# Attention over picked rows in the second layer: scores in four row tiles of TensorE, scaling on GpSimd, another order of turning and projecting

## The chip, the cores and the metric

One core of a Trainium2 chip runs the whole program. The metric is the device time of one execution in microseconds; where a median is given, it is over several executions of the same kernel. The engines are TensorE (PE, with its weight loads as PEld), VectorE (DVE), ScalarE (ACT), GpSimd (POOL) and the queue of SyncE (SP), which issues most DMA transfers.

## The reference

Two samples of 128 rows with 512 columns pass through two layers of a perceiver: cross-attention, attention, feed-forward, and the same again. Six stages follow one another. The change touches one, the cross-attention of the second layer, which picks one context row for each row of x and then attends over the picked rows:

```python
def _L1_xattn_ref(q, kv, Wq, Wkv, Wc):        # q: 2 x 128 x 512, kv: 2 x 2048 x 512, 16 heads of 32
    qp = jnp.einsum('bld,ed->ble', q, Wq)
    scores = jnp.einsum('bld,bmd->blm', qp, kv)
    idx = jnp.argmax(scores, axis=-1)
    mem = jnp.take_along_axis(kv, idx[..., None], axis=1)      # the picked rows
    mkv = jnp.einsum('bld,ed->ble', mem, Wkv)                  # one key and one value of 32, shared by the heads
    mk, mv = jnp.split(mkv, 2, axis=-1)
    qh = qp.reshape(b, l, h, dh).transpose(0, 2, 1, 3)
    logits = jnp.einsum('bhld,bmd->bhlm', qh, mk) * scale
    attn = jax.nn.softmax(logits, axis=-1)
    out = jnp.einsum('bhlm,bmd->bhld', attn, mv)
    return jnp.einsum('bld,ed->ble', out.transpose(0, 2, 1, 3).reshape(b, l, d), Wc)

x = x + _L1_xattn_ref(_layernorm(x, axis=-1), ctx_1024, L1_xattn_Wq, L1_xattn_Wkv, L1_xattn_Wc)
```

## The kernel before, in words

Each engine has its own program, written out by hand in the order in which it runs; semaphores join them. No planner moves anything, so the order of calls in `cross1_pe`, `cross1_act`, `cross1_dve` and in the GpSimd and SyncE blocks is the order on the chip. Everything in this stage runs in float32; such a matmul leaves two records in the trace, a transposing one leaves one.

The stage works on two samples, b = 0 and 1. For each it does the following.

1. The scores over 2048 context rows go to four PSUM banks, DVE finds the largest (`pick_dve`), and GpSimd fetches the picked rows with an indirect DMA (L2692).
2. TensorE turns them (`turn_mem`, L2035), `copy_mem` (L2141, on ACT) brings them to SBUF, and `project_mem` makes the key (L2041) and the value (L2045). The key weights stand four times side by side, so that the key appears in each of the four groups of 32 partitions.
3. `spread_mk` (DVE, L2214) multiplies the key with a mask, so that `mkz` holds four blocks, each with the key in one group of 32 partitions and zeros in the others. With it `logits` (L2053) makes the scores of four heads in one matmul of 128 partitions by 512 columns, one bank for each group of four heads (heads 4j to 4j+3 in bank j), and signals after each bank.
4. For each bank j, DVE takes the maxima (`largest_la`, L2220 and L2221), ACT the exponentials with their sums (`exp_la`, L2151), DVE the reciprocals (L2226) and the scaling (L2227), both in `scale_la`. TensorE turns the scaled weights (`turn_la`, L2059), a copy brings them back (`copy_laT`: DVE L2231 for sample 0, ACT L2168 for sample 1), and `mix_mem` (L2065) multiplies with the value.
5. `out_x1` (L2069) multiplies with the output weights, which lie in the ring block `BLK_X1 + 1`, and DVE adds the result to x (L2267, L2271).

`keep_clock` (L275) are matmuls without use, put where TensorE would wait. The ring has four blocks of 1 MB, which SP refills from `stream` through `dma_block` (L222) once `blk_used` says that the one before is spent. The context comes back to SBUF through eight transfers that GpSimd issues (L2689). Behind this stage comes `linear_pe` (L2305), and then the feed-forward with its large matmuls (L2470, L2487, L2488).

Of the kernel before, what the change touches and what calls it, by code (L numbers as in the profile page):

```python
# [16 lines left out]
P = 128  # L17
B = 2
D = 512
C = D // P  # L20
# [6 lines left out]
DK = D // H  # L27
# [6 lines left out]
RING = 4  # L34
# [81 lines left out]
def build(nc, x, ctxT, ctx_rows, wq, wk, wv, wo, stream, small, cols, rows, consts, out):  # L116
# [6 lines left out]
    with ExitStack() as ctx:  # L123
# [43 lines left out]
        def view(at, *shape, one_pass=False):  # L167
            n = int(np.prod(shape))
            assert at + n <= ARENA, (at, shape)
            if one_pass:  # L170
                assert at // ARENA_R == (at + n - 1) // ARENA_R, (at, shape)
                v = arena_r[at // ARENA_R][:, at % ARENA_R:at % ARENA_R + n]
            else:
                v = arena[:, at:at + n]
            if len(shape) == 1:
                return v
            letters = "abcd"[:len(shape)]
            return v.rearrange(f"p ({' '.join(letters)}) -> p {' '.join(letters)}",
                               **dict(zip(letters[:-1], shape[:-1])))
# [1774 lines left out]
        mkz = view(19456, B, 4, P)  # L1954
# [30 lines left out]
        mkz_ready = sem("mkz_ready")  # L1985
        mv_ready = sem("mv_ready")
# [13 lines left out]
        X1_BANK = (5, 6)  # L2000
        CTX_SPLITS = ctx_count(B - 1, KB - 1, 0)
        LA_SCALE = float(1.0 / np.sqrt(DK).astype(np.float32))

        def cross1_pe(pe):
# [44 lines left out]
            def logits(b):  # L2049
                pe.wait_ge(mkz_ready, b + 1)  # L2050
                pe.wait_ge(mv_ready, b + 1)
                for j in range(C):
                    nc.tensor.matmul(psum[:, PICK_BANK[b] + j, :], qpT[:, j, b * P:(b + 1) * P], mkz[:, b, :, :],  # L2053
                                     start=True, stop=True).then_inc(la_filled, 1)
# [30 lines left out]
            turn_mem(1)  # L2085
            project_mem(1)
            logits(1)
            for j in range(C):
                turn_la(0, j)
            for j in range(C):  # L2090
                last = mix_mem(0, j, psum[:, PICK_BANK[0], j * P:(j + 1) * P])
            last.then_inc(x1o_filled, 1)
            need(pe, BLK_X1 + 1)
# [17 lines left out]
        def cross1_act(act):  # L2111
# [30 lines left out]

            def copy_mv(b):
                act.wait_ge(mkv_filled, 2 * b + 2)
                nc.scalar.copy(mvt[:, b, :], psum[:, MV_BANK[b], 0:DK]).then_inc(mv_ready, 1)
# [8 lines left out]

            copy_mem(0)
            copy_mv(0)
            exp_la(0, 0)
            exp_la(0, 1)
            copy_mem(1)
            exp_la(0, 2)  # L2160
# [19 lines left out]
            copy_x1o(C - 1)  # L2180

        def cross1_dve(dve):
# [29 lines left out]
            def spread_mk(b):  # L2212
                dve.wait_ge(mkv_filled, 2 * b + 1)
                nc.vector.tensor_tensor(mkz[:, b, :, :], per_row(psum[:, MK_BANK[b], 0:P], 4),  # L2214
                                        per_elem(K_("headmask", 0, 4), P), ALU.mult).then_inc(mkz_ready, 1)

            def largest_la(b, j):
                dve.wait_ge(la_filled, C * b + j + 1)
                heads = slice(4 * j, 4 * j + 4)
                link(dve, nc.vector.reduce_max(lm[:, b, heads], bank4(PICK_BANK[b] + j), AX.X))  # L2220
                nc.vector.tensor_scalar(nlm[:, b, heads], lm[:, b, heads], -LA_SCALE, None, ALU.mult).then_inc(lm_ready, 1)  # L2221

            def scale_la(b, j):
                dve.wait_ge(la_exp, C * b + j + 1)
                heads = slice(4 * j, 4 * j + 4)
                link(dve, nc.vector.reciprocal(ls[:, b, heads], ls[:, b, heads]))  # L2226
                nc.vector.tensor_tensor(la[:, b, heads, :], la[:, b, heads, :], per_elem(ls[:, b, heads], P), ALU.mult).then_inc(la_ready, 1)  # L2227
# [19 lines left out]
            spread_mk(0)  # L2247
            for j in range(C):
                largest_la(0, j)
            scale_la(0, 0)  # L2250
            spread_mk(1)
            scale_la(0, 1)
            largest_la(1, 0)
            largest_la(1, 1)
            scale_la(0, 2)
            largest_la(1, 2)
            largest_la(1, 3)
            scale_la(0, 3)
            for j in range(C):
                copy_laT(0, j)  # L2260
            scale_la(1, 0)
            dve.wait_ge(x1o_filled, 1)
            nc.vector.tensor_copy(x1oT[:, :, 0:P], bank4(PICK_BANK[0])).then_inc(x1o_ready, 1)
            for j in range(1, C):
                scale_la(1, j)
# [322 lines left out]
        def _(sp):  # L2588
# [74 lines left out]
            with sp.Fori(0, E) as e:  # L2663
                for q, (u, i) in enumerate(MOE_ORDER):
                    dma_block(sp, ds(e * NEXP + (BLK_MOE + 3 * u + i), 1), BLK_MOE + q, used=e * NEXP + (BLK_MOE + q - RING + 1))
            turns = (NBLK - BLK_X1) // RING
            with sp.Fori(0, turns) as i:
                for s in range(RING):
                    dma_block(sp, ds(i * RING + (BLK_X1 + s), 1), BLK_X1 + s, used=i * RING + (BLK_X1 + s - RING + 1))
# [8 lines left out]
        def _(gp):  # L2678
# [11 lines left out]
            for b in range(B):  # L2690
                gp.wait_ge(picked, b + 1)
                gp.indirect_dma_start(out=mem[:, b, :], out_offset=None, in_=ctx_rows,  # L2692
                                      in_offset=bass.IndirectOffsetOnAxis(ap=pick[b][:, :], axis=0)).then_inc(mem_arrived[b], 16)
# [102 lines left out]
```

## Time and profile before

| | us |
|---|---|
| median of three runs | 1342.53 |
| the three runs | 1336.44, 1345.71, 1342.53 |
| profiled execution, device time | 1338.34 |
| profiled execution, span of the trace | 1336.6 |
| PE busy in the span | 1301.4 |
| DVE busy | 916.7 |
| ACT busy | 718.3 |
| GpSimd busy | 28.6 |

The span is that of the trace, the device time also holds what lies around it. Busy times come from single records; the end of a matmul in them is modelled. The changed code works between about 1012 us and 1046 us of the span.

### The profile page before, as it was taken

The numbers are of one execution on the slowest core, as the hardware profiler recorded it, in microseconds if no ns is written. First come the engines' busy times: TensorE is split into PE (matmuls) and PEld (weight loads), VectorE is DVE, ScalarE is ACT, GpSimd is POOL, SyncE is SP. The second block draws the span as 40 slices with busy tenths as digits, with TensorE's granted clock in tenths as the row PEclk, the third lists the DMA queues.
The fourth block names the chain that finished last, engine by engine and source line by source line (L and its number), as shares of the span: only waits on it lengthen the run. The fifth ranks groups of instructions, "written<-read, shape, count | busy, mean of one in ns | idle before, by whom it ended". The sixth has DMA issues, their size and how long they took to land.

```text
span 1336.6 us, 23941 instructions
## 1 busy us (share of the span) xinstructions
PE 1301.4 (97%) x9964; PEld 1104.9 (83%) x9964; DVE 916.7 (69%) x1199; ACT 718.3 (54%) x888; POOL 28.6 (2%) x24
## 2 busy tenths in 40 slices
PE   9999999999999999998999999999988999999998
PEld 8899998989999997776677888888765789888887
DVE  4566566776565665675688989989868577555554
ACT  5544444554444443482377777777654445666552
POOL 0000000000000000002000000000011010000000
PEclk9999999999999999997899999999989999999999
DMA  8101010321010011201069999999970145455552
GB/s 298 37 23 45 23 37 21 107 75 37 21 37 26 23 64 64 95 34 66 33 225 343 349 361 350 344 351 349 364 269 16 64 158 187 174 190 191 189 191 90
DMA packets 50367, 197.72 MB, mean 148 GB/s; under 512 B 12128, under 2 KB 20576, under 8 KB 30560
## 3 DMA queue, kind: packets, MB, share of 16 engines
q1 hardware_dynamic: 47936, 187.41, 39.0%
q0 software_dynamic: 2336, 8.91, 1.8%
q8 instruction: 75, 1.23, 0.4%
q14 instruction: 20, 0.16, 0.0%
HBM read 195.78 MB, written 0.52 MB: 147 GB/s over the span
## 4 chain that ended last, share of the span: by engine, by line
PE 88%; DVE 6%; ACT 2%; DMA 2%; issue 2%; SPq 0%; POOL 0%; ACTq 0%; DVEq 0%
PE psum L465 13%; PE psum L435 13%; PE psum L2487 9%; PE psum L1683 8%; PE psum L492 5%; PE psum L2488 4%; PE psum L1706 4%; PE psum L517 4%; PE psum L1686 4%; PE psum L2470 3%; PE psum L1053 2%; PE psum L1709 2%; PE psum L2496 2%; PE psum L476 1%; PE psum L1720 1%
## 5 line engine op out<-in xcount | busy, mean ns | idle before, releaser
L1752 DVE TENSOR_TENSOR arena_r<-ring,arena_r 128x2048 fp32r<-128x2048 f32 x96 | 219.7, 2290 | 29.5 <-ACT arena_r L1746 29.2
L465 PE MATMUL psum<-ring_r,arena_r 128*128 128x256 f32 x1536 | 198.1, 287 | 0.6 <-DVE ring_r L300 0.6
L1746 ACT CAST arena_r<-ring 128x2048 fp32r<-128x2048 f32 x96 | 183.4, 1914 | 14.4 <-PE psum L1686 11.1
L465 PEld LDWEIGHTS psum<-ring_r,arena_r 128*128 128x128 f32 x1536 | 188.6, 191 | 1.3 <-DVE ring_r L300 1.0
L435 PE MATMUL psum<-arena_r 128*128 128x512 f32 x768 | 184.0, 394 | 0.8 <-ACT arena_r L809 0.4
L2487 PE MATMUL psum<-arena_r 128*128 128x512 f32 x512 | 177.7, 393 | 1.1 <-DVE arena_r L2562 1.1
L435 PEld LDWEIGHTS psum<-arena_r 128*128 128x128 f32 x768 | 141.5, 188 | 33.3 <-issue 1.6
L2488 PE MATMUL psum<-arena_r 128*128 128x256 f32 x512 | 142.6, 279 | 0.0
L2441 DVE TENSOR_TENSOR arena_r<-ring,arena_r 128x2048 fp32r<-128x2048 f32 x43 | 98.6, 2293 | 62.1 <-ACT arena_r L2436 62.1
L1683 PE MATMUL psum<-arena_r 128*128 128x512 f32 x512 | 129.5, 395 | 1.3 <-issue 1.3
L2487 PEld LDWEIGHTS psum<-arena_r 128*128 128x128 f32 x512 | 95.9, 187 | 22.9 <-DVE arena_r L2562 1.3
L1683 PEld LDWEIGHTS psum<-arena_r 128*128 128x128 f32 x512 | 94.2, 188 | 20.4 <-issue 1.7
L795 ACT COPY arena<-psum 128x1024 f32<-128x1024 f32 x64 | 61.7, 1016 | 89.6 <-PE psum L492 89.6
L300 DVE TENSOR_TENSOR arena_r<-arena,arena_r 128x2048 fp32r<-128x2048 f32 (+4 forms) x34 | 52.1, 1538 | 80.8 <-ACT arena_r L766 52.3
L2436 ACT CAST arena_r<-ring 128x2048 fp32r<-128x2048 f32 x44 | 84.0, 1910 | 30.0 <-PE psum L2470 19.7
L2488 PEld LDWEIGHTS psum<-arena_r 128*128 128x128 f32 x512 | 96.5, 188 | 0.0
L650 DVE TENSOR_TENSOR arena<-arena,psum 128x1024 f32<-128x1024 f32 x64 | 75.2, 1216 | 24.8 <-PE psum L506 24.8
L787 ACT COPY ring<-psum 128x512 f32<-128x512 f32 x64 | 37.2, 581 | 77.8 <-PE psum L465 77.8
L802 ACT ACTIVATE arena<-arena 128x1024 f32<-128x1024 f32 x64 | 66.3, 1058 | 21.0 <-DVE arena L650 19.7
L630 DVE TENSOR_TENSOR arena<-arena 128x512 f32<-128x512 f32 x124 | 69.3, 559 | 4.2
L1686 PE MATMUL psum<-arena_r 128*128 128x512 f32 x256 | 68.5, 390 | 0.0
L492 PEld LDWEIGHTS psum<-arena 64*128 64x128 f32 x1024 | 59.7, 188 | 9.9 <-issue 9.1
(345 smaller groups left out, 1902.7 us busy)
## 6 DMA issues: line engine op xcount, KB each, us to landing
ring<-in_stream SPq DMA_DIRECT2D x151, 1024.0 KB, 4.9
arena<-in_ctxT POOLq DMA_DIRECT2D x8, 1024.0 KB, 11.9
arena<-in_ctxT SPq DMA_DIRECT2D x7, 1024.0 KB, 8.1
arena<-in_wk SPq DMA_DIRECT2D x16, 256.0 KB, 3.2
wv_in<-in_wv SPq DMA_DIRECT2D x8, 512.0 KB, 3.6
arena<-in_wq SPq DMA_DIRECT2D x16, 256.0 KB, 2.7
arena<-in_wk SPq DMA_DIRECT2D x16, 128.0 KB, 3.2
arena<-in_wo SPq DMA_DIRECT2D x2, 1024.0 KB, 6.9
```

The source lines that it names most:

```text
L435: last = nc.tensor.matmul(bank, wk_sb[wp][:, c, w], cx[xp][kb][:, c, :], start=c == wp == xp == 0, stop=c == C - 1 and xp == 1)
L465: last = nc.tensor.matmul(bank[:, q * T:(q + 1) * T], cx[xp][kc // 4][:, c, kc % 4 * P:(kc % 4 + 1) * P], wv_sb[wp][:, c, :], start=c == w ...
L492: last = nc.tensor.matmul(psum[:, 2 * half + kc // 4, kc % 4 * P:kc % 4 * P + P], kT[j % 2][a:a + 64, k0:k0 + P], qT[a:a + 64, j % 2, half ...
L650: nc.vector.tensor_tensor(part, part, per_row(psum[:, SPREAD_BANK, 0:P], KC // 2), ALU.subtract).then_inc(shifted, 1)
L1683: nc.tensor.matmul(out, xg[xp][:, c, e, :], hi[:, c, :], start=c == xp == 0, stop=False)
L1686: last = nc.tensor.matmul(out, xg[0][:, c, e, :], lo[:, c, :], start=False, stop=c == C - 1)
L1746: nc.scalar.copy(mwhi[p % MB], ring[k % RING][:, :]).then_inc(moe_hi, 1)
L1752: nc.vector.tensor_tensor(mwlo[p % MB], ring[(BLK_MOE + p) % RING][:, :], mwhi[p % MB].bitcast(fp32), ALU.subtract).then_inc(moe_lo if p < ...
L2436: nc.scalar.copy(whi[j % 2], ring[k % RING][:, :]).then_inc(w_hi, 1)
L2441: nc.vector.tensor_tensor(wlo[j % 2], ring[(BLK_W12 + j) % RING][:, :], whi[j % 2].bitcast(fp32), ALU.subtract).then_inc(w_lo, 1)
L2487: nc.tensor.matmul(psum[:, 4 + s, :], w[0][:, c, :], src[:, :, c, :], start=c == 0, stop=False)
L2488: last = nc.tensor.matmul(psum[:, 4 + s, 0:T], w[1][:, c, :], src[:, 0, c, :], start=False, stop=c == FC - 1)
```

## The change

The mask is gone. `copy_mk` (ACT) copies the key from PSUM as it is (128 x 128), and `logits` makes 16 matmuls, each with 32 partitions of the query and of the key and 128 columns: row group j of the array writes to bank j, head group c to its column block. So bank j now holds the heads j, 4+j, 8+j and 12+j, and `la_filled` is raised once, after all 16. As the heads stand in another order, the rows of the output weights must too: SP loads block `BLK_X1 + 1` in four transfers of 32 partitions, each with runs of 512 numbers in place of 2048, and the first turn of its last loop is written out for that.

The scaling goes from DVE to GpSimd (`cross1_pool`), the reciprocals stay on DVE (`sums_la`). The copy of the second sample's picked rows goes from ACT to DVE. On TensorE `turn_la(0, 0)` comes ahead of `project_mem(1)` and `turn_la(0, 1)` ahead of `logits(1)`; the wait for the output weights moves ahead of `mix_mem` of sample 0.

```diff
             def logits(b):
-                pe.wait_ge(mkz_ready, b + 1)
-                pe.wait_ge(mv_ready, b + 1)
-                for j in range(C):
-                    nc.tensor.matmul(psum[:, PICK_BANK[b] + j, :], qpT[:, j, b * P:(b + 1) * P], mkz[:, b, :, :],
-                                     start=True, stop=True).then_inc(la_filled, 1)
+                pe.wait_ge(mkv_ready, 2 * b + 2)
+                for c in range(C):
+                    for j in range(4):
+                        r = tile_rows(j)
+                        last = nc.tensor.matmul(psum[:, PICK_BANK[b] + j, c * P:(c + 1) * P], qpT[r, c, b * P:(b + 1) * P], mk[r, b, :],
+                                                start=True, stop=True)
+                last.then_inc(la_filled, 1)
...
             logits(0)
             turn_mem(1)
+            turn_la(0, 0)
             project_mem(1)
+            turn_la(0, 1)
             logits(1)
-            for j in range(C):
+            for j in range(2, C):
                 turn_la(0, j)
+            need(pe, BLK_X1 + 1)
+            pe.wait_ge(wo_arrived, WO_PARTS * 16)
             for j in range(C):
                 last = mix_mem(0, j, psum[:, PICK_BANK[0], j * P:(j + 1) * P])
             last.then_inc(x1o_filled, 1)
-            need(pe, BLK_X1 + 1)
             turn_la(1, 0)
...
+            def copy_mk(b):
+                act.wait_ge(mkv_filled, 2 * b + 1)
+                nc.scalar.copy(mk[:, b, :], psum[:, MK_BANK[b], 0:P]).then_inc(mkv_ready, 1)
...
             copy_mem(0)
+            copy_mk(0)
             copy_mv(0)
-            exp_la(0, 0)
-            exp_la(0, 1)
-            copy_mem(1)
-            exp_la(0, 2)
+            for j in range(3):
+                exp_la(0, j)
+            copy_mk(1)
             copy_mv(1)
             exp_la(0, 3)
...
+        def cross1_pool(gp):
...
+            for b in range(B):
+                for j in range(C):
+                    heads = slice(4 * j, 4 * j + 4)
+                    gp.wait_ge(ls_ready, C * b + j + 1)
+                    nc.gpsimd.tensor_tensor(la[:, b, heads, :], la[:, b, heads, :], per_elem(ls[:, b, heads], P), ALU.mult).then_inc(la_ready, 1)
...
-            def scale_la(b, j):
+            def sums_la(b, j):
                 dve.wait_ge(la_exp, C * b + j + 1)
                 heads = slice(4 * j, 4 * j + 4)
-                link(dve, nc.vector.reciprocal(ls[:, b, heads], ls[:, b, heads]))
-                nc.vector.tensor_tensor(la[:, b, heads, :], la[:, b, heads, :], per_elem(ls[:, b, heads], P), ALU.mult).then_inc(la_ready, 1)
+                nc.vector.reciprocal(ls[:, b, heads], ls[:, b, heads]).then_inc(ls_ready, 1)
...
+            dma_block(sp, BLK_X1, BLK_X1, used=BLK_X1 - RING + 1)
+            sp.wait_ge(blk_used, BLK_X1 - RING + 2)
+            for i in range(4):
+                part = stream[BLK_X1 + 1].rearrange("(j d) (c n) -> d j c n", d=DK, c=C)[:, :, i, :]
+                sp.dma_start(block(BLK_X1 + 1)[tile_rows(i), :, :], part).then_inc(wo_arrived if i else blk_arrived[(BLK_X1 + 1) % RING], 16)
+            for k in range(BLK_X1 + 2, BLK_X1 + RING):
+                dma_block(sp, k, k, used=k - RING + 1)
             turns = (NBLK - BLK_X1) // RING
-            with sp.Fori(0, turns) as i:
+            with sp.Fori(1, turns) as i:
```

On TensorE, from the end of the picking to the mixing of sample 0, there stood before (L2035 turns picked rows, L2041 and L2045 project, L2053 makes scores, L2059 turns weights, L2065 mixes):

```order
L2053 MATMUL psum<-arena 128x512 x4
L2035 MATMUL psum<-cst,arena 128x128 x4
L2041 MATMUL psum<-arena,sml 128x128 x4
L2045 MATMUL psum<-sml,arena 128x32 x4
L2053 MATMUL psum<-arena 128x512 x4
L2059 MATMUL psum<-cst,arena 128x128 x16
```

and now stands, with L2055 for the scores, L2036 and L2062 for the turning, L2042 and L2046 for the projecting:

```order
L2055 MATMUL psum<-arena 128x128 x16
L2036 MATMUL psum<-cst,arena 128x128 x4
L2062 MATMUL psum<-cst,arena 128x128 x4
L2042 MATMUL psum<-arena,sml 128x128 x4
L2046 MATMUL psum<-sml,arena 128x32 x4
L2062 MATMUL psum<-cst,arena 128x128 x4
L2055 MATMUL psum<-arena 128x128 x16
L2062 MATMUL psum<-cst,arena 128x128 x8
```

Two of the four groups of turned weights of sample 0 moved up, one ahead of the projecting of sample 1 and one ahead of its scores.

On DVE, from the last maxima of sample 0 on, the rows before were these (L2214 spreads the key, L2226 and L2227 scale, L2231 copies turned weights, L2263 copies the mixed values of sample 0):

```order
L2226 RECIPROCAL ls<-ls 128x4
L2227 TENSOR_TENSOR arena<-arena,ls 128x512
L2214 TENSOR_TENSOR arena<-psum,col 128x512
L2226 RECIPROCAL ls<-ls 128x4
L2227 TENSOR_TENSOR arena<-arena,ls 128x512
L2220 TENSOR_REDUCE lm<-psum 128x4
L2221 TENSOR_SCALAR nlm<-lm 128x4
L2220 TENSOR_REDUCE lm<-psum 128x4
L2221 TENSOR_SCALAR nlm<-lm 128x4
L2226 RECIPROCAL ls<-ls 128x4
L2227 TENSOR_TENSOR arena<-arena,ls 128x512
```

and now they are these (L2246 takes the reciprocals, L2235 copies the picked rows of sample 1, L2250 copies turned weights, L2240 and L2241 take the maxima):

```order
L2246 RECIPROCAL ls<-ls 128x4
L2235 COPY arena<-psum 128x4x128
L2246 RECIPROCAL ls<-ls 128x4 x2
L2250 COPY arena<-psum 128x512 x2
L2246 RECIPROCAL ls<-ls 128x4
L2240 TENSOR_REDUCE lm<-psum 128x4
L2241 TENSOR_SCALAR nlm<-lm 128x4
L2240 TENSOR_REDUCE lm<-psum 128x4
```

The scalings left this engine, and the maxima of sample 1 now stand behind the reciprocals of the last bank of sample 0 and behind two copies.

## Rows read from the trace of the kernel before

**Rows 1.** The page: busy time by engine, then the engines' shares of the chain.

```profile
PE 1301.4 (97%) x9964; PEld 1104.9 (83%) x9964; DVE 916.7 (69%) x1199; ACT 718.3 (54%) x888; POOL 28.6 (2%) x24
PE 88%; DVE 6%; ACT 2%; DMA 2%; issue 2%; SPq 0%; POOL 0%; ACTq 0%; DVEq 0%
```

**Rows 2.** Chain that ended last, 1017 to 1046: start, length, work.

```profile
1017.42 0.70 DVE lm L2220
...
1018.36 2.90 ACT arena L2151 x16
1021.25 0.48 ACT arena L2141
...
1021.78 1.16 PE psum L2041 x8
1022.94 0.83 PE psum L2045 x8
...
1023.79 0.19 ACT mvt L2145
...
1024.12 1.11 PE psum L2053 x2
...
1025.25 0.70 DVE lm L2220
...
1030.22 2.40 DVE arena L2231 x4
...
1032.73 0.70 DVE arena L2227
...
1033.57 1.09 PE psum L2059 x4
1034.66 1.71 PE psum L2069 x2
...
1036.83 0.86 PE psum L2069 x2
...
1038.63 0.86 PE psum L2069 x2
...
1043.06 2.79 PE psum L2069 x6
```

**Rows 3.** Timeline, 1015 to 1021: start, length, engine, line, work.

```profile
1015.38 0.98 POOL L2692 DMA_INDIRECT arena<-in_ctx_rows,pick  x1 [5.43 <-DVE pick L2210]
...
1016.29 3.67 PE L2053 MATMUL psum<-arena 128*128 128x512 f32 x8
...
1018.28 0.69 DVE L2220 TENSOR_REDUCE lm<-psum 128x4 f32<-128x512 f32 x1
...
1019.80 0.60 PE L2035 MATMUL psum<-cst,arena 128*128 128x128 f32 x4
```

**Rows 4.** Timeline of the mixer stage: 16 matmuls of 32 partitions, four row groups.

```profile
614.96 1.17 PE L1083 MATMUL psum<-arena 32*128 32x128 f32 x32
...
622.80 1.70 PE L1083 MATMUL psum<-arena 32*128 32x128 f32 x32 [2.73 <-DVE arena L1373]
```

**Rows 5.** Groups on GpSimd, by form: busy time, mean ns of one.

```profile
L1379 POOL TENSOR_TENSOR arena<-arena 128x1024 f32<-128x1024 f32 x4 | 9.3, 2346 | 67.5 <-ACT arena L1334 67.5
...
L2695 POOL TENSOR_TENSOR arena_r<-ring,arena_r 128x2048 fp32r<-128x2048 f32 x1 | 4.5, 4547 | 55.1 <-ACT arena_r L2436 55.1
```

**Rows 6.** Windows: length, busy PE, PEld, DVE, ACT, POOL; then PEclk, DMA share, GB/s.

```profile
973.00:974.00 1.00, 0.00 (x0) 0.00 (x0) 0.93 (x4) 0.50 (x3) 1.00 (x2) 1.00 0.11 33
...
975.00:976.00 1.00, 0.36 (x1) 0.36 (x2) 0.28 (x1) 1.00 (x2) 1.00 (x3) 0.50 0.97 279
...
980.00:981.00 1.00, 1.00 (x4) 0.82 (x3) 0.81 (x1) 0.00 (x0) 0.00 (x0) 0.50 1.02 381
...
1028.00:1032.00 4.00, 2.56 (x31) 1.60 (x28) 3.90 (x10) 3.87 (x23) 0.00 (x0) 1.00 0.00 0
1032.00:1036.00 4.00, 3.37 (x22) 1.79 (x23) 3.86 (x11) 0.58 (x1) 0.00 (x0) 0.61 0.00 0
```

More of the change, by code:

```diff
@@ L1953, in build @@
         memT = view(18432, C, T)
-        mkz = view(19456, B, 4, P)
+        mk = view(19456, B, P)
         la = view(20480, B, H, P)
@@ L1984, in build @@
         mkv_filled = sem("mkv_filled")
-        mkz_ready = sem("mkz_ready")
-        mv_ready = sem("mv_ready")
+        mkv_ready = sem("mkv_ready")
+        ls_ready = sem("ls_ready")
         la_filled = sem("la_filled")
@@ L2000, in build @@
         X1_BANK = (5, 6)
+        WO_PARTS = 2 + 3
         CTX_SPLITS = ctx_count(B - 1, KB - 1, 0)
@@ L2141, in copy_mem @@
                 nc.scalar.copy(memT[:, :, b * P:(b + 1) * P], bank4(MEM_BANK[b])).then_inc(memT_ready, 1)
+            def copy_mk(b):
+                act.wait_ge(mkv_filled, 2 * b + 1)
+                nc.scalar.copy(mk[:, b, :], psum[:, MK_BANK[b], 0:P]).then_inc(mkv_ready, 1)
             def copy_mv(b):
                 act.wait_ge(mkv_filled, 2 * b + 2)
-                nc.scalar.copy(mvt[:, b, :], psum[:, MV_BANK[b], 0:DK]).then_inc(mv_ready, 1)
+                nc.scalar.copy(mvt[:, b, :], psum[:, MV_BANK[b], 0:DK]).then_inc(mkv_ready, 1)
             def exp_la(b, j):
@@ L2180, in cross1_act @@
             copy_x1o(C - 1)
+        def cross1_pool(gp):
+            for b in range(B):
+                gp.wait_ge(picked, b + 1)
+                gp.indirect_dma_start(out=mem[:, b, :], out_offset=None, in_=ctx_rows,
+                                      in_offset=bass.IndirectOffsetOnAxis(ap=pick[b][:, :], axis=0)).then_inc(mem_arrived[b], 16)
+            for b in range(B):
+                for j in range(C):
+                    heads = slice(4 * j, 4 * j + 4)
+                    gp.wait_ge(ls_ready, C * b + j + 1)
+                    nc.gpsimd.tensor_tensor(la[:, b, heads, :], la[:, b, heads, :], per_elem(ls[:, b, heads], P), ALU.mult).then_inc(la_ready, 1)
         def cross1_dve(dve):
@@ L2210, in pick_dve, with copy_mem @@
                 nc.vector.tensor_scalar(pick[b][:, :], at8[b][:, 0:1], b * CTX, None, ALU.add).then_inc(picked, 1)
[L2212 to L2215, printed above, removed]
+            def copy_mem(b):
+                dve.wait_ge(memT_filled, b + 1)
+                nc.vector.tensor_copy(memT[:, :, b * P:(b + 1) * P], bank4(MEM_BANK[b])).then_inc(memT_ready, 1)
             def largest_la(b, j):
-                dve.wait_ge(la_filled, C * b + j + 1)
+                dve.wait_ge(la_filled, b + 1)
                 heads = slice(4 * j, 4 * j + 4)
@@ L2246, in cross1_dve @@
             pick_dve(1)
-            spread_mk(0)
             for j in range(C):
                 largest_la(0, j)
[L2250 to L2258, printed above, removed]
+            sums_la(0, 0)
+            copy_mem(1)
+            sums_la(0, 1)
+            sums_la(0, 2)
+            copy_laT(0, 0)
+            copy_laT(0, 1)
+            sums_la(0, 3)
             for j in range(C):
-                copy_laT(0, j)
-            scale_la(1, 0)
+                largest_la(1, j)
+            copy_laT(0, 2)
+            copy_laT(0, 3)
+            sums_la(1, 0)
             dve.wait_ge(x1o_filled, 1)
@@ L2264, in cross1_dve @@
             for j in range(1, C):
-                scale_la(1, j)
+                sums_la(1, j)
             dve.wait_ge(x1_proj, 2)
@@ L2689, in _ @@
                     gp.dma_start(ctxT_sb[b][kb], ctxT[b][:, :, kb * 512:(kb + 1) * 512]).then_inc(ctx_back[(b * KB + kb) // 2], 16)
[L2690 to L2693, printed above, removed]
+            cross1_pool(gp)
             gp.wait_ge(w_hi, 1)
```

## The prediction

> **What bounds the kernel now.** The page says first where a gain could lie at all: PE is busy in 97% of the span and holds 88% of the chain that ended last [rows 1]. The changed stage is some 34 us of 1336.6, from 1012 to 1046, so nothing in it can move the total by more than a small part. Then I read the chain through this stage [rows 2]. It changes hands at each step: maxima on DVE, exponentials on ACT (two banks in 2.90 us), the copy of sample 1's picked rows (1021.25), projecting (1021.78, 1022.94), the value's copy (1023.79), scores of sample 1 (1024.12), maxima (1025.25), then DVE without a break until the scaling at 1032.73. From 1033.57 to 1045.85 (1043.06 + 2.79) TensorE runs alone, turning and multiplying for sample 1. So two thirds of the stage is latency, one third PE's own work. Last I read the clock by windows [rows 6]: full in 1028 to 1032, 0.61 in 1032 to 1036.
>
> **The change part by part.** I follow sample 0 and then sample 1 through the new order, with the durations of the old trace.
>
> *Scores.* The old four matmuls took 3.67 us, and DVE began on the first bank 1.13 us after their start (1016.29 to 1017.42) [rows 2, 3]. The new form, 16 matmuls of 32 partitions into four banks, stands in the mixer: 1.17 us for the 16 (32 records) [rows 4]. With about 0.07 us to the next engine all four banks are there after 1.24 us. PE gets 2.5 us back per sample, but DVE takes a bank each 0.86 us (1017.42 to 1018.28) [rows 2, 3], as fast as PE made them before. Sample 0's maxima start at 1017.53 and end at 1020.97: no gain, 0.1 us lost.
>
> *The mask.* `spread_mk` was one DVE pass over a bank, about 0.7 us by the others of that size [rows 2], made while PE was still making the value and ACT copying it, so it lay beside other work; `copy_mk` takes its place there. Worth nothing for the chain.
>
> *Picked rows of sample 1.* PE turned them at 1019.80 [rows 3], behind the scores. The issue of the gather ends at 1016.36 (1015.38 + 0.98) [rows 3], and the rows had landed when PE came for them, so the landing lies between; I take 1018.9. The exact time is of no weight, since DVE, which copies now, is in the maxima until 1020.97; it then takes a reciprocal (0.2) and copies a bank (0.7): 1021.87. Before, ACT's copy let PE go at 1021.78. Nothing gained.
>
> *Turning ahead of projecting.* PE now waits at `turn_la(0, 0)` with `project_mem(1)` queued behind it, and behind that ACT's `copy_mv(1)` and with it `exp_la(0, 3)`. It waits for GpSimd's first scaling. GpSimd's two-input operation takes 2346 ns at 1024 columns and 4547 at 2048 [rows 5], that is 2.15 ns a column and 0.15 us fixed: 1.25 us at 512. From the reciprocal at 1021.15: done at 1022.45, turned by 1022.95. So projecting starts at 1022.95 in place of 1021.78: 1.2 us late. From its start to that of the scores it took 2.34 us (1021.78 to 1024.12) [rows 2]: scores at 1025.3.
>
> *Maxima of sample 1.* They need the banks (1026.5) and stand behind `sums_la(0, 3)`, whose exponentials start after `copy_mv(1)` at 1025.15 and take 1.5: 1026.9, where it was 1025.25. Then DVE has four maxima (3.44), two copies of turned weights (1.2, half of the four in 2.40 [rows 2]) and a reciprocal (0.2): 4.9 us, to 1031.8. Before, the same point was reached 7.4 us after 1025.25, at 1032.6, since three scalings and four copies lay between. This is the gain: 2.5 us less on DVE, of which 1.65 is spent on the late start. GpSimd scales in 1.25, and `turn_la(1, 0)` starts at 1033.2 where it was 1033.57 [rows 2]: 0.4 us early.
>
> *Tail.* Turning, multiplying and mixing for one group take PE 1.80 us at full clock (1036.83 to 1038.63 [rows 2]); GpSimd delivers each 1.25 us, so PE stays the bound and the tail keeps its length. At full clock throughout it would be shorter: `out_x1` took 1.71 at first and 0.86 later, the first turning 1.09 in place of about 0.6 [rows 2], so 1.2 us are the low clock's [rows 6].
>
> *Output weights in four transfers.* They go out where the DMA engines have a share of only 0.11 soon after (973 to 974) [rows 6], before the last six context transfers, and are needed at 1031. Cover: some 50 us. If it were gone, some of the block's 1 MB at 0.38 MB/us (380 GB/s) [rows 6] would stand on the path, up to 2.6 us.
>
> *The clock.* This is what the latency sum leaves out. PE's work in the middle shrinks by 5 us. From 1017.5 to 1022.5 it has only the 0.6 us of turning left [rows 3]. Two stretches show what follows. PE idle at 973 to 974 had the clock at 0.50 by 975, and still there at 980 with PE fully busy [rows 6]. And 1028 to 1032, with PE busy 2.56 of 4 us, was followed by 0.61. So I expect the clock to fall near 1021, ahead of `project_mem(1)`. At half, projecting (1.16 + 0.83) takes 2.0 more, the scores 1.70 in place of 1.17 [rows 4]: `turn_la(1, 0)` moves from 1033.2 to about 1035.3, or 1.7 later than before. Against that, a clock that has come back by the tail saves up to 1.2 there.
>
> The Trainium skill, "TensorE: Matmul & The Clock Gate", Part 4, says that a transpose does not count as PE being busy in the way a matmul does. By that rule the turning in the gap does not hold the clock and the fall is surer; if turning counted in full, nothing above would change but the chance.
>
> **The sum.** With the clock as before: -0.4 us. With a fall in the gap: +1.7, less 0 to 1.2 in the tail, so +0.5 to +1.7, and up to +2.9 if the low clock also reaches 1.2 us deeper into the tail than it did. I take the second case at +1.0: profiled execution 1338.34 + 1.0 = 1339.3. The three timed runs lie 9 us apart; their middle is 1342.53, the mean of all four executions is 1340.8. From the latter I forecast 1342, no change that can be measured (about 1% or 13 us is what a measurement tells from none).
>
> **The rivals.**
>
> *The clock holds.* Then -0.4, or -1.6 if it holds in the tail too: 1340. For it: in 1028 to 1032 PE was idle for 1.44 of 4 us and the clock stayed full throughout [rows 6]. Against: the new gap is three times that.
>
> *GpSimd becomes the bound, ending slower.* The scaling reads its second operand spread over 128 columns, a form that is not in the trace. If it took the 2.35 us of a 1024-column one, the first turning and with it projecting would come 1.1 late, `turn_la(1, 0)` 1.1 more, and the tail would be paced by GpSimd: three times 2.35 - 1.80, 1.6 us. Together +3.8 on the sum: 1345. It decides from 1.80 us for one scaling. The linear price of 1.25 [rows 5] speaks against.
>
> The Trainium skill, "GPSIMD Engine Reference", Engine selection, says to keep elementwise work of two inputs on VectorE, since GpSimd is about twice slower. By that factor DVE's 0.69 would become an estimate of 1.4 us, 0.15 above mine, still under 1.80; the rule's warning holds for each operation but not for this place, where DVE is the fuller engine.
>
> *The row groups don't run side by side.* Then 16 matmuls take the old 3.7 us and the one signal comes at their end: maxima of sample 0 start 2.5 late, everything on behind it, and the same for sample 1. +4 to +5: 1346. The mixer's 1.17 us [rows 4] speaks against; it is the same shape and bank pattern.
>
> *More is gained than the chain shows.* PE's 5 us of freed work could count only if PE were what the middle waits for, and it is not. The most that the stage could give back is the 2.5 us of DVE and the 1.2 of the clock: 1338.
>
> **How the numbers follow.** Chances: fall of the clock in the gap, +0.5 to +2.9, 0.55; clock holds, 0.27; GpSimd paces, 0.08; row groups serial, 0.03; more gained, 0.07. All of them lie within 6 us of 1341, well inside 1%, so "same" gets 0.95; the rest, 0.03 faster and 0.02 slower, is for something outside this stage that no row shows. The range takes the lowest run (1336.4) less 1.6 and the highest (1345.7) plus 2.9: 1335 to 1349; three runs' spread makes nearly all of it.
>
> **What would show it.** Right: the new scores at about 1.2 us with four row groups overlapping; GpSimd's scaling at 1.2 to 1.4 us; `project_mem(1)` waiting for the turning behind GpSimd, starting some 10.4 us after `turn_mem(0)`; a granted clock under 1 between the scores of sample 0 and those of sample 1; the stage (from `turn_mem(0)` to the last addition) within 3 us of its 33.3. Wrong: a stage more than 3 us shorter, which would mean that DVE's order costs less than I sum; scaling above 1.8 us; or a difference outside 1012 to 1046, above all in the context transfers before 983, which the four new transfers could delay.

## The result, and the profile after

The changed kernel is slower by a third of a per cent: 1347.28 us median of 15 runs (1344.61 to 1350.16) against 1342.53 us of 15 runs of the kernel before (1336.44 to 1349.17), ratio 1.0032 with a 95% interval of 1.0019 to 1.0044. That is inside the range that was given, but the interval leaves out "no change", and no move was forecast.

The two profiled executions lie 10.2 us apart (spans 1336.6 and 1346.8), twice the difference of the medians. So the first step was to cut both spans at landmarks and to see which pieces belong to the change.

| piece (us) | before | after | difference |
|---|---|---|---|
| start to the first matmul of the experts (L1612) | 668.5 | 669.8 | 1.3 |
| from there to the first turning of picked rows | 344.1 | 346.7 | 2.6 |
| the stage, from that turning to the last addition to x | 33.3 | 36.2 | 2.9 |
| middle of the feed-forward (L2487, L2505 to the last product) | 177.6 | 181.0 | 3.4 |

A second trace of the kernel before (n1, below) has 180.9 us for the last row with the same code, and 666.6 for the first. The first and the last row are therefore differences between executions, and 5.5 us are left for the change, close to the 4.75 us of the medians. The trace of before is the odd one: over all 14 traces the last row is 181.0 in twelve (180.97 to 180.99), 179.2 in e7 and 177.6 in this one alone.

The stage first. The chain that ended last in the changed kernel answers to [rows 2] (start, length, work):

```profile
1021.50 0.70 DVE lm L2240
...
1024.95 1.04 POOL arena L2201
...
1026.04 1.11 PE psum L2062 x4
1027.16 1.71 PE psum L2042 x8
1028.86 1.55 PE psum L2046 x8
1030.41 0.91 PE psum L2062 x4
1031.32 2.06 PE psum L2055 x32
...
1033.40 0.70 DVE lm L2240
...
1036.69 1.19 DVE arena L2250 x2
...
1038.04 1.05 POOL arena L2201
...
1039.13 1.12 PE psum L2062 x4
1040.25 1.71 PE psum L2072 x2
...
1042.81 1.71 PE psum L2072 x2
...
1049.89 2.79 PE psum L2072 x6
```

The reader is to see two things. GpSimd's scaling (L2201) stands on the chain twice, at 1.04 us each. And every TensorE step of the chain between 1026 and 1043 is stretched: the key takes 1.71 us where it took 1.16, the value 1.55 for 0.83, turning 1.1, the scores of sample 1 2.06, and two `out_x1` (L2072) take 1.71 where only one did.

The windows say why (columns as in [rows 6]; the seventh number after the length is the granted clock as a share):

```profile
1020.00:1024.00 4.00, 1.44 (x34) 0.98 (x32) 2.39 (x7) 2.89 (x11) 0.45 (x1) 1.00 0.25 70
1024.00:1028.00 4.00, 3.07 (x13) 2.68 (x14) 2.48 (x7) 2.73 (x16) 2.70 (x3) 0.50 0.00 0
1028.00:1032.00 4.00, 4.00 (x29) 3.67 (x31) 0.65 (x1) 1.82 (x10) 0.37 (x1) 0.50 0.00 0
1032.00:1036.00 4.00, 3.38 (x52) 2.71 (x44) 2.71 (x9) 1.70 (x11) 1.04 (x1) 0.72 0.00 0
1036.00:1040.00 4.00, 1.95 (x20) 1.23 (x21) 2.77 (x8) 4.00 (x24) 1.53 (x2) 0.70 0.00 0
1040.00:1044.00 4.00, 4.00 (x10) 1.80 (x8) 0.18 (x1) 1.19 (x3) 2.54 (x3) 0.50 0.02 4
```

After 1020 to 1024, where PE is busy for 1.44 of 4 us, the clock is at half (1.2 in place of 2.4 GHz) for ten microseconds; it comes back, PE idles again around 1036, and it halves a second time, into the tail. Before, there was one such stretch [rows 6].

The timeline of the changed kernel shows the new scores and the gap behind them (start, length, engine, line; idle time before and its end in brackets):

```profile
978.47 1.22 PE L275 MATMUL psum<-cst 128*128 128x256 f32 x2 [4.65 <-issue]
...
1020.26 1.17 PE L2055 MATMUL psum<-arena 32*128 32x128 f32 x32
...
1024.33 1.11 PE L2036 MATMUL psum<-cst,arena 128*128 128x128 f32 x4 [2.89 <-DMA arena<-in_ctx_rows,pick]
```

The scores take 1.17 us, to the digit what the mixer's took [rows 4]; then TensorE has nothing for 2.89 us. The first line is the other piece: TensorE stands still for 4.65 us near 975, 3.17 in the trace before, ahead of an instruction that waits for no semaphore. "Issue" means that the profile names no releaser.

### The profile page after: what moved, and what is told of

Its sections match the earlier page's. It is cut to its first block, busy times and chain, and to the rows that moved or that the text cites. A ratio compares the mean times of both kernels' runs of the same rounds, so it can differ in the third digit from the quotient of the medians.

```text
span 1346.8 us, 24025 instructions
## 1 busy us (share of the span) xinstructions
PE 1307.5 (97%) x10012; PEld 1111.6 (83%) x10012; DVE 910.9 (68%) x1190; ACT 718.4 (53%) x889; POOL 36.7 (3%) x32
## 4 chain that ended last, share of the span: by engine, by line
PE 88%; DVE 6%; ACT 2%; DMA 2%; issue 2%; POOL 0%; SPq 0%; ACTq 0%; DVEq 0%
PE psum L465 13%; PE psum L435 13%; PE psum L2505 9%; PE psum L1683 8%; PE psum L492 5%; PE psum L2506 4%; PE psum L1706 4%; PE psum L517 4%; PE psum L1686 4%; PE psum L2488 3%; PE psum L1053 2%; PE psum L1709 2%; PE psum L2514 2%; PE psum L476 1%; PE psum L1720 1%
## 5 line engine op out<-in xcount | busy, mean ns | idle before, releaser
L2505 PE MATMUL psum<-arena_r 128*128 128x512 f32 x512 | 181.0, 399 | 1.1 <-DVE arena_r L2580 1.1
L2505 PEld LDWEIGHTS psum<-arena_r 128*128 128x128 f32 x512 | 96.2, 188 | 25.3 <-DVE arena_r L2580 1.2
## 6 DMA issues: line engine op xcount, KB each, us to landing
arena<-in_ctxT POOLq DMA_DIRECT2D x8, 1024.0 KB, 13.1
```

Source lines behind the costliest of these rows:

```text
L2505: nc.tensor.matmul(psum[:, 4 + s, :], w[0][:, c, :], src[:, :, c, :], start=c == 0, stop=False)
```

## The experiments

All traces, cut in the same way (us, to within 0.1; the stage ends where the last addition starts). "Wait" is that idle time near 975; "rows" the time from L1612 to the first turning of picked rows; "value" and "maxima" when the last matmul of sample 1's value and its last maximum start, from the stage's start; "tail" from the first `out_x1` to the last addition.

| trace | load in | wait | rows | stage | value | maxima | tail |
|---|---|---|---|---|---|---|---|
| before | one | 3.17 | 344.1 | 33.3 | 10.9 | 15.9 | 11.4 |
| n1, before again | one | 3.05 | 345.3 | 32.1 | 10.9 | 16.0 | 10.6 |
| after | four narrow | 4.65 | 346.7 | 36.2 | 13.5 | 19.3 | 12.7 |
| e1 | one | 3.20 | 343.9 | 36.0 | 13.5 | 19.3 | 12.4 |
| e2 | four narrow | 4.38 | 347.9 | 32.1 | 10.9 | 16.0 | 10.6 |
| e3 | one | 3.06 | 345.1 | 31.1 | 11.9 | 16.7 | 10.5 |
| e4 | one | 3.62 | 345.1 | 35.1 | 12.8 | 18.9 | 10.6 |
| e5 | one | 3.57 | 345.4 | 33.3 | 12.5 | 17.8 | 10.5 |
| e6 | one | 2.81 | 345.2 | 33.9 | 13.1 | 18.9 | 11.2 |
| e7 | one | 3.12 | 347.1 | 31.8 | 11.6 | 16.4 | 11.2 |
| e8 | one | 3.07 | 345.1 | 30.1 | 10.9 | 15.7 | 10.5 |
| e9 | one | 3.59 | 345.2 | 31.0 | 11.5 | 16.6 | 10.5 |
| e10 | four of all partitions | 3.26 | 344.1 | 32.1 | 10.9 | 15.9 | 10.6 |
| e11 | four narrow, long runs | 4.93 | 349.1 | 32.0 | 10.8 | 15.9 | 10.6 |

### e1: the changed kernel with one transfer

The rows of the output weights are put in the new order when the arrays are laid out, and SP's loop is the old one.

```diff
-    mats += [a["L1_xattn_Wq"].T, a["L1_xattn_Wc"].T]
+    wc = a["L1_xattn_Wc"].T
+    mats += [a["L1_xattn_Wq"].T, wc.reshape(C, 4, DK, D).transpose(1, 0, 2, 3).reshape(D, D)]
...
-            pe.wait_ge(wo_arrived, WO_PARTS * 16)
...
-            for i in range(4):
-                part = stream[BLK_X1 + 1].rearrange("(j d) (c n) -> d j c n", d=DK, c=C)[:, :, i, :]
-                sp.dma_start(block(BLK_X1 + 1)[tile_rows(i), :, :], part)...
...
-            with sp.Fori(1, turns) as i:
+            with sp.Fori(0, turns) as i:
```

> The changed kernel, with the output weights' rows put in the new order when the arrays are laid out, so that one transfer of 1 MB loads the block and the loop of the queue is the old one. Load theory: of the loss of 4.7 us the four transfers hold some 2.5 (the wait of TensorE before its turning at about 975 us goes from 4.65 back to 3.2, and the context arrives 1 us sooner), so 1344.5 to 1345.5. Clock theory alone: the loss stays, 1347, and the stage from turning the picked rows to the last addition stays at 36.2 us. Drift theory (the rest lies in the feed-forward, in code that did not change): 1347 with a feed-forward middle near 181 us again.

Measured: 1346.79 us median, ratio to the kernel before 1.0009 (0.9992 to 1.0026). The interval takes in no change, and the 12 runs are scattered (1337.22 to 1348.64). The ratio has come down from 1.0032, but its interval overlaps that of the changed kernel, and the median lies only 0.5 us under 1347.28, where the load theory had some 2.5. So the times do not settle it. The trace is plainer: the wait is 3.20, the rows piece 343.9, and the stage is 36.0, as in the changed kernel.

### e2: the kernel before with four transfers

```diff
+            pe.wait_ge(wo_arrived, WO_PARTS * 16)
...
+            dma_block(sp, BLK_X1, BLK_X1, used=BLK_X1 - RING + 1)
+            sp.wait_ge(blk_used, BLK_X1 - RING + 2)
+            for i in range(4):
+                part = stream[BLK_X1 + 1].rearrange("(j d) (c n) -> d j c n", d=DK, c=C)[:, :, i, :]
+                sp.dma_start(block(BLK_X1 + 1)[tile_rows(i), :, :], part)...
...
```

The arrays are laid out so that the same block results.

> The kernel before, with the block of output weights loaded by four transfers of 32 partitions and the array laid out so that the block is the same. Load theory: slower than before by 1.5 to 3 us (1344 to 1345.5), rate of the DMA engines near 230 GB/s for several us before 972, the stage itself unchanged at 33.2. Clock theory alone: as before, 1342.5.

Measured: 1346.01 us, ratio 1.0014 (0.9997 to 1.0031). Wait 4.38, rows piece 347.9, stage 32.1. The interval just takes in no change. In the trace the transfers bring the wait with them into the old kernel, and leave the stage alone.

### n1: the kernel before once more

No edit.

> The kernel before, once more, for its trace. If the middle of the feed-forward (177.6 us before, 181.0 in the changed kernel, same code) differs from run to run by a few us, the drift theory holds and those 3.4 us are not of the change; if it is 177.6 again, they are.

Measured: 1339.88 us, middle of the feed-forward 180.9 us. The drift theory holds: those 3.4 us are not of the change. The trace also shows the old stage at 32.1 in place of 33.3, with the clock full throughout. e2, e10 and e11 have 32.0 to 32.1 too, so the low stretch on which [rows 6] rests was in one of five traces of the old stage.

### e10 and e11: which feature of the four transfers is slow

Both are the kernel before. e10 cuts the block by columns (all 128 partitions, runs of 2 KB), e11 by partitions (32 each, runs of 8 KB).

```diff
+                part = stream[BLK_X1 + 1][:, i * D:(i + 1) * D]                 # e10
+                dst = block(BLK_X1 + 1)[:, i, :]
...
+                part = stream[BLK_X1 + 1][tile_rows(i), :]                      # e11
+                dst = ring[(BLK_X1 + 1) % RING][tile_rows(i), :]
```

> The kernel before, with the block of output weights in four transfers of all 128 partitions and 512 numbers each: short runs of 2 KB, all partitions. If the short runs make the load slow, TensorE's wait near 975 us is 4.4 us as with the four transfers of 32 partitions, and the engines move under 300 GB/s for some us before; if not, 3.1 us and about 400 GB/s.

> The kernel before, with the block of output weights in four transfers of 32 partitions, each row whole: 8 KB runs. If writing to 32 partitions at a time makes the load slow, TensorE's wait near 975 us is 4.4 us and the rate is under 300 GB/s; if not, 3.1 us and about 400 GB/s.

Measured: wait 3.26 and 4.93, rows piece 344.1 and 349.1; one execution each, 1344.35 and 1349.42. The window 970 to 975, first of e10, with 388 GB/s at a DMA share of 1.00:

```profile
970.00:975.00 5.00, 4.59 (x20) 3.25 (x19) 1.44 (x2) 1.97 (x2) 0.00 (x0) 1.00 1.00 388
```

and of e11, with the engines as busy and 225 GB/s:

```profile
970.00:975.00 5.00, 4.59 (x20) 3.24 (x19) 1.24 (x2) 1.97 (x2) 0.00 (x0) 1.00 1.04 225
```

The changed kernel has 229 in the same place, e1 422 (the windows of those two):

```profile
968.00:973.00 5.00, 4.59 (x19) 3.25 (x19) 1.82 (x3) 1.97 (x2) 0.00 (x0) 1.00 1.10 229
```

```profile
970.00:975.00 5.00, 4.59 (x20) 3.16 (x18) 2.40 (x4) 1.97 (x2) 0.00 (x0) 1.00 1.02 422
```

It is the 32 partitions, not the short runs. The Trainium skill, "SBUF — State Buffer", Door 1, says that DMA bandwidth depends on how many of the 16 ports a transfer's partitions reach, and that a group of 32 reaches eight of them. By that rule the rate should halve, and it nearly does, 388 to 225; the order in which four such transfers share the ports is not in the traces.

What TensorE waits for near 975 can be read from the `--dma` view, which counts packets by queue and has queues of the kind "instruction" (packets, MB, share of the engines' time). Seven microseconds around the wait, 970.7 to 977.7 in the kernel before and 972 to 979 in the changed one, give the same two lines:

```profile
q8 instruction: 1, 0.02, 1.0%
q14 instruction: 1, 0.01, 0.3%
```

The packet of queue 8 has 16 KB and takes 1.1 us. One falls into the wait in each of the 14 traces, and TensorE's next matmul starts 1.42 to 1.46 us after its end. What differs is when it starts: 0.3 to 1.1 us after TensorE stopped in the eleven traces with a wide load, 1.8 to 2.4 us in the three with a narrow one (in the changed kernel TensorE stopped at 973.82 and the packet started at 975.92; before, 972.47 and 973.13).

### e3: fillers in both gaps

e1 with matmuls without use where TensorE stood idle:

```diff
             logits(0)
+            pe.wait_ge(picked, 2)
+            keep_clock(pe, 3, 5)
             turn_mem(1)
+            keep_clock(pe, 3, 3)
             turn_la(0, 0)
...
             for j in range(C):
+                if j == 2:
+                    keep_clock(pe, 5, 4)
                 last = mix_mem(0, j, psum[:, PICK_BANK[0], j * P:(j + 1) * P])
             last.then_inc(x1o_filled, 1)
+            keep_clock(pe, 5, 2)
```

> As the kernel with one transfer, and matmuls without use in the gaps that the change opened on TensorE: 5 and 3 around the turning of the second sample's picked rows, 4 and 2 around the end of the mixing of sample 0. Clock theory: granted clock 1.0 through the stage, projecting of sample 1 back at 2.0 us in place of 3.3, the stage at 31.5 to 33 us in place of 36.2, total 3 to 4.5 us under the run with one transfer. Rival (the stage is held by GpSimd and the order, not by the clock): the stage within 1 us of 36.2. Rival (the fillers stand in the way themselves): longer than 36.2.

Measured: 1342.72 us, ratio to the kernel before 0.9993 (0.9980 to 1.0007), 4.1 us under e1's median in the same job (by the two ratios, 2.1); stage 31.1. The windows of e1, two of them with the clock at 0.50:

```profile
1019.00:1023.00 4.00, 1.44 (x34) 1.25 (x35) 2.77 (x7) 2.91 (x12) 0.12 (x1) 0.88 0.26 70
1023.00:1027.00 4.00, 3.07 (x15) 2.67 (x14) 2.10 (x7) 2.35 (x14) 3.09 (x3) 0.50 0.00 0
1027.00:1031.00 4.00, 4.00 (x35) 3.67 (x37) 0.87 (x2) 1.86 (x10) 0.05 (x1) 0.50 0.00 0
```

and of e3, whose stage begins at the same 1015.1:

```profile
1019.00:1023.00 4.00, 3.39 (x42) 2.66 (x42) 2.79 (x7) 2.91 (x12) 0.13 (x1) 1.00 0.26 70
1023.00:1027.00 4.00, 3.82 (x29) 3.62 (x30) 2.08 (x7) 2.59 (x15) 3.07 (x3) 1.00 0.00 0
1027.00:1031.00 4.00, 3.15 (x51) 2.46 (x54) 2.68 (x7) 2.30 (x14) 1.04 (x1) 1.00 0.00 0
```

The edit adds matmuls and one wait to TensorE and nothing else, and takes 4.9 us off the stage. This is the clearest of the runs: the low clock cost all that the stage lost and more. The clock is not a matter of the profiled execution alone: the granted clock over the whole program is 0.981 on average in the timed runs of the changed kernel and of e1, 0.986 in those of e3 and of the kernel before. The gain in time, 2.1 to 4.1 us, is less sharp than that of the stage.

### e7: fillers in the first gap alone

e3 without the second pair:

```diff
             for j in range(C):
-                if j == 2:
-                    keep_clock(pe, 5, 4)
                 last = mix_mem(0, j, psum[:, PICK_BANK[0], j * P:(j + 1) * P])
             last.then_inc(x1o_filled, 1)
-            keep_clock(pe, 5, 2)
```

> The kernel with one transfer and with fillers around the turning of picked rows alone (5 and 3 matmuls), none at the mixing of sample 0. Clock theory: value projected at about 11.9 us and last maxima at 16.7 as with all fillers (13.5 and 19.3 without), then the clock halves at the second gap and the tail is 12 to 12.7 us in place of 10.5: stage 32.5 to 33.5, between 31.1 and 36.0.

Measured: 1342.74 us (0.9990, 0.9968 to 1.0013); value at 11.6, maxima at 16.4, tail 11.2, stage 31.8. The clock falls in the second gap (0.99 in 1032 to 1036, 0.58 in the next four microseconds). The first gap holds 4.2 of the 4.9 us, the second 0.7, less than the 1.4 to 2.4 that I expected.

### e4: the tiled scores alone

The kernel before with the row tiles, the key copied by ACT, one signal after 16 matmuls, one transfer. Old order, scaling on DVE.

```diff
-                for j in range(C):
-                    nc.tensor.matmul(psum[:, PICK_BANK[b] + j, :], qpT[:, j, b * P:(b + 1) * P], mkz[:, b, :, :],
-                                     start=True, stop=True).then_inc(la_filled, 1)
+                for c in range(C):
+                    for j in range(4):
+                        r = tile_rows(j)
+                        last = nc.tensor.matmul(psum[:, PICK_BANK[b] + j, c * P:(c + 1) * P], qpT[r, c, b * P:(b + 1) * P], mk[r, b, :],
+                                                start=True, stop=True)
+                last.then_inc(la_filled, 1)
```

> The kernel before with the scores in four row tiles alone (ACT copies the key, no mask, one signal after 16 matmuls, output weights laid out for it): the old order, scaling on DVE. The stage is counted from the first turning of picked rows to the last addition to x (32.1 to 33.3 us before, 36.0 to 36.2 changed). Clock theory (2.5 us less work per sample leave TensorE idle after the scores, the clock halves, projecting runs at half speed): granted clock under 1 within 12 us of the stage's start, stage 34 to 35.5 us. Order theory (the wait for GpSimd ahead of projecting is what costs): clock full, stage 32 to 32.8.

Measured: 1343.70 us (1.0001, 0.9977 to 1.0025), stage 35.1, and the clock at half from 1020 on, where the stage began at 1012.5:

```profile
1016.00:1020.00 4.00, 1.46 (x34) 0.98 (x32) 2.37 (x7) 2.89 (x11) 0.53 (x1) 0.94 0.25 70
1020.00:1024.00 4.00, 3.03 (x13) 2.63 (x14) 2.33 (x7) 3.35 (x17) 0.00 (x0) 0.50 0.00 0
```

The faster scores, with the key's copy on ACT and one signal in place of four, bring the fall of the clock and a stage 3 us longer than n1's, with no other part of the change in place. The total did not move measurably; ten runs resolve 3 us barely.

### e5: turning back behind the scores of sample 1

e1 with PE's old order, and DVE's copies of sample 0 behind the maxima of sample 1:

```diff
             turn_mem(1)
-            turn_la(0, 0)
             project_mem(1)
-            turn_la(0, 1)
             logits(1)
-            for j in range(2, C):
+            for j in range(C):
                 turn_la(0, j)
...
-            copy_laT(0, 0)
-            copy_laT(0, 1)
             sums_la(0, 3)
             for j in range(C):
                 largest_la(1, j)
-            copy_laT(0, 2)
-            copy_laT(0, 3)
+            for j in range(C):
+                copy_laT(0, j)
```

> The changed kernel with one transfer, and the turning of sample 0 back behind the scores of sample 1 (on DVE its four copies behind the maxima of sample 1). Scaling stays on GpSimd. Clock theory: the gap after the scores is there all the same, clock under 1, value of sample 1 projected 13 us after the start (13.5 in the changed kernel, 10.9 before), stage 35 to 36.5. Order theory: value projected at 11 to 11.5, stage 33 or less.

Measured: 1342.39 us (0.9999, 0.9969 to 1.0030), stage 33.3, value at 12.5, maxima at 17.8. Neither theory as put: the clock fell as the one said (0.50 from 1020 to 1028), but the stage is 2.7 us shorter than e1's and well under the 35 that it had; the other had a value at 11 to 11.5. Projecting started a microsecond sooner, and the second fall did not come (tail 10.5 for 12.4).

### e6 and e9: scaling back on DVE, without and with fillers

```diff
-                nc.vector.reciprocal(ls[:, b, heads], ls[:, b, heads]).then_inc(ls_ready, 1)
+                link(dve, nc.vector.reciprocal(ls[:, b, heads], ls[:, b, heads]))
+                nc.vector.tensor_tensor(la[:, b, heads, :], la[:, b, heads, :], per_elem(ls[:, b, heads], P), ALU.mult).then_inc(la_ready, 1)
```

GpSimd's loop over the banks goes.

> The changed kernel with one transfer and with the scaling back on DVE. GpSimd theory (each scaling of 1.0 us and its hand-overs stand on the path): stage 1 to 2 us shorter than 36.0. Clock theory: the gap remains, DVE is fuller again by 0.7 us a bank, stage 36 to 37.5.

> The kernel with one transfer and fillers in both gaps, with the scaling on DVE. At the clock of the filled kernel this prices GpSimd alone. GpSimd theory (it costs some 1 us on the path, as 36.0 against 33.9 without fillers suggested): stage 30.1. Clock theory (those 2 us were two stretches of low clock that fell otherwise): stage 31 to 32.

Measured: e6 1344.35 us (1.0017, 0.9993 to 1.0042), stage 33.9, where GpSimd's form has 36.0. e9 1343.20 us (0.9997, 0.9981 to 1.0014), stage 31.0, where GpSimd's form (e3) has 31.1. At a steady clock the engine that scales makes no difference; 1.2 of the 2.1 us between e1 and e6 lie in the tail, where the second stretch of low clock is longer in e1 (0.59 and 0.56 in 1035 to 1043, against 0.61 and 1.00 in e6). By trace alone e6 would have been read as the price of GpSimd.

### e8: fillers, and projecting ahead of the first turning

```diff
             turn_mem(1)
-            keep_clock(pe, 3, 3)
-            turn_la(0, 0)
+            keep_clock(pe, 3, 1)
             project_mem(1)
+            turn_la(0, 0)
             turn_la(0, 1)
```

> The kernel with one transfer and fillers in both gaps, with projecting of sample 1 ahead of the first turning of weights (one filler matmul between them in place of three). If the wait for GpSimd ahead of projecting costs what it showed, the value is projected 0.8 us sooner than the 11.9 of the filled kernel and the stage falls from 31.1 to about 30.3, total 1342 (0.5 to 1 under the filled one, 1.5 to 2 under the kernel before). If the maxima of sample 1 are held by something else (exponentials of the last bank of sample 0), the stage stays at 31.1.

Measured: 1340.17 us (1335.51 to 1342.27, 12 runs) against 1342.53, ratio 0.9975 (0.9958 to 0.9991); stage 30.1. It is the one version whose interval lies below both kernels, the one before at 1 and the changed one at 1.0032. The stage is 1.0 us under e3's, so the turning ahead of projecting, with its wait for GpSimd, cost about what the sum had for it (1.2). Its TensorE timeline from the scores of sample 0 to those of sample 1:

```profile
1017.31 1.17 PE L2055 MATMUL psum<-arena 32*128 32x128 f32 x32
1018.41 2.42 PE L275 MATMUL psum<-cst 128*128 128x256 f32 x10
1021.41 0.66 PE L2036 MATMUL psum<-cst,arena 128*128 128x128 f32 x4 [0.57 <-DMA arena<-in_ctx_rows,pick]
...
1022.85 1.16 PE L2042 MATMUL psum<-arena,sml 128*128 128x128 f32 x8 [0.35 <-DVE arena L2240]
...
1025.65 1.17 PE L2055 MATMUL psum<-arena 32*128 32x128 f32 x32
```

Scores at 1.17 us twice, projecting 1.16 us, no idle time over 0.6 us.

Two parts of the change were not run alone: the copy of the picked rows on DVE, and the wait for the output weights ahead of `mix_mem`.

## Why the prediction was wrong, step by step

**The sign.** The forecast was +1.0 on the stage and nothing elsewhere, and no change overall. It failed in two terms: that of the clock was mis-sized (+1.0 in place of +2.9), and that of the output weights was put at nothing (2.8 in the traces, of which 1.6 stand clear of their scatter).

**The clock (right mechanism, size off).** The middle came as worked out: the fall ahead of `project_mem(1)`, its start at 10.4 us (1026.95 less 1016.51), the turning of sample 1 at 22.6 us from the stage's start, where the sum gave 22.7 (1035.3 less 1012.62). That both agree to 0.1 is in part luck. GpSimd was 0.2 us faster than priced, and the turnings ran at half clock (1.1 us where the sum had 0.5). The price of the scores at half clock, 1.70, came from a row in which the clock was 0.64 on average; at 0.50 they took 2.09.

The tail did not come as worked out. I took 0 to 1.2 us off for a clock that would be back by then; a second fall at 1038 stretched two groups, and from that turning to the last addition went 13.6 us (1039.13 to 1052.70) in place of 12.3. The case was "up to +2.9" and the stage lost 2.9; against n1's clean 32.1 it is 4.1, since the old trace had already one low stretch that the four others lack. I set the middle of the case on a hope for the tail, and measured from a trace whose own clock was not the usual one. What e3 shows is that low clock held 4.9 us of e1's stage, all of it avoidable. With the clock full the sum had 31.7 (33.3 less 1.6), and e3 has 31.1: without the clock the sum was 0.6 us off.

**Output weights in four transfers (missed).** The step said that they go out where the DMA engines have a share of 0.11 and that some 50 us cover them. The block's own deadline was far indeed. But SP issued them at 959.76 with the engines full, so each microsecond more that they take pushes back what is queued behind, and the gap of 0.11 at 973 to 974 was the slack that they ate: in the changed kernel the share while TensorE waits (974 to 975) is 1.04. It was priced at 380 GB/s, the rate of transfers to 128 partitions; to 32 at a time it is 225 to 240. The prediction did name a delay before 983 as a sign of being wrong, but gave it no term. Three traces with narrow transfers have 347.9 us on average for the rows piece, eleven without 345.1: 2.8 us (one of the eleven, e7, has 347.1, so single traces overlap).

Two parts make up the difference. The first is TensorE's wait near 975 (4.4 to 4.9 in place of 2.8 to 3.6): from the start of the last matmul of L1667 to the first one that makes the query (L2009, L2010 in the changed kernel) the narrow traces take 9.9 to 10.7 us and the others 8.3 to 9.4, 1.6 us on average and without overlap. The second is the picking up to the first turning: 34.4 to 36.5 us against 33.1 to 36.8, which overlap. This second part goes with the clock again. It takes 33.1 to 33.3 us in the three traces whose granted clock from 986 to 1006 is 1.00 (before, e1 and e10), 33.9 to 35.2 in the eight with 0.91, and 36.0 to 36.8 in the three with 0.83 (e2, e7 and e11). Two of these three have the narrow load; whether it brings the lower clock about is open.

The wait is for instructions, as far as the traces can say: its end follows that of an instruction packet by the same 1.42 to 1.46 us in all 14, and the packet starts late where the narrow load stands ahead. The view does not name the engine that a queue serves. The Trainium skill, "Runtime: NRT & Kernel Launch", Instruction fetch mechanics, says that each engine's sequencer fetches its code in blocks through a DMA queue of its own; the packet of 16 KB fits that.

The times bear the split out only roughly: e1 has 1.0009 and e2 1.0014, and both intervals take in no change.

**The four rivals.** The clock did not hold. GpSimd did not become the bound: its scaling took 1.04 us, under the 1.25 of the linear price, and e9 against e3 prices it at nothing. The spread second operand did not make it dearer than the linear price; what it costs by itself no run shows. The Trainium skill, "GPSIMD Engine Reference", Engine selection, has GpSimd about twice slower at work of two inputs; here 0.69 against 1.04 is a factor of 1.5. The row groups ran side by side at 1.17 us. More gained: not in this kernel. e8's stage is 3.2 us under the 33.3 of before, within the 3.7 that this rival had, but only 2.0 under n1's, and its total is 1340.17, not 1338 (1340.8 less 3.7 would have been 1337).

**The base.** I took 1340.8 as the level of the kernel before; 15 runs put it at 1342.53. That is 1.7 us of the miss of 5.3.

## What to carry to other kernels

Work taken off an engine that is not the bound can cost time where the engine's clock falls in the idle time that it leaves: before making TensorE's part of a latency-bound stage cheaper, mark the idle stretches that appear and say what fills them. A transfer's price is what it pushes back in a queue that is full when it is issued, not whether its own deadline is far; and a load cut into groups of 32 partitions ran at little over half the rate here (225 to 240 GB/s), while one cut along the columns ran at 388. Where the array can be laid out beforehand, a new row order costs nothing on the chip: with one transfer the wait is 3.20 us as in the kernel before. And two profiled executions should be cut at landmarks and set beside a repeat before their difference is read: 3.4 of 10.2 us lay in code that nobody had touched.

## What the runs showed of the hardware

- Four loads into 32 partitions each kept the DMA engines fully busy at 225 to 240 GB/s; four of all 128 partitions with 2 KB runs reached 388, a single one 422.
- The clock halved after four microseconds in which PE was busy for 1.44 (the scores of sample 0 and what was left of the work ahead of them), and stayed at half for ten microseconds although PE was fully busy for most of them (1028 to 1032: 4.00 of 4).
- Sixteen float32 matmuls of 32 partitions and 128 columns in four row groups took 1.17 us at the full clock and 2.09 at half (1031.24 to 1033.33 in the changed kernel).
- GpSimd's two-input multiply of 128 x 512 with a spread operand took 1.03 to 1.04 us alone, where 2346 ns for 1024 columns [rows 5] had suggested 1.25; VectorE's took 0.69.
- The same loops of the feed-forward took 181.0 us in twelve traces, 179.2 in one and 177.6 in one, with a median of 398, 395 and 392 ns for the matmuls of L2487 and its counterparts, all at a granted clock of 1.00; what differs is open.
- In 14 of 14 traces a wait of TensorE for no semaphore (2.8 to 4.9 us) ended 1.42 to 1.46 us after a packet of 16 KB on an instruction queue; the packet started 0.3 to 1.1 us into the wait, or 1.8 to 2.4 where narrow loads filled the DMA engines.
